# Attention over the keys inside a streaming loop: TensorE sums the weighed values, VectorE normalises the probabilities first and does its pieces of work in another order

## The reference

```python
# B, E, G, P = 64, 16, 5000, 128
W = weight * mask[None, :, :]
h = jnp.einsum('bg,egp->bep', x, W) + bias[None, :, :]
# attention on the normed rows
scores = jnp.einsum('bhqd,bhkd->bhqk', q, k) * scale
scores = jnp.where(mask, scores, jnp.finfo(scores.dtype).min)
attn = jax.nn.softmax(scores, axis=-1)
out = jnp.einsum('bhqk,bhkd->bhqd', attn, v)
h = h + out.transpose(0, 2, 1, 3).reshape(b, s, d) @ W_o.T
# then: top 2 of 64 experts for each row of the normed h, plus two shared experts
```

## Time and profile before

| | |
|---|---|
| median of 3 runs (lowest, highest) | 241.35 us (240.23, 242.11) |
| profiled execution | 241.4 us, span 239.7 us |
| TensorE busy | 184.3 us, 77% |
| VectorE busy | 152.4 us, 64% |
| GpSimd busy | 145.6 us, 61% |
| ScalarE busy | 82.7 us, 35% |
| mean granted TensorE clock | 0.953 of full speed |

### The profile page before, as it was taken

The page is one execution under the profiler, slowest core; times in us unless marked ns, Lnnn a source line. Parts: engine busy times, 40 slices in busy tenths (PEclk is TensorE's granted clock), DMA queues, the critical chain, the costliest instruction groups (busy, mean ns, idle before and its releaser), DMA issues.

```text
span 239.7 us, 6216 instructions
## 1 busy us (share of the span) xinstructions
PE 184.3 (77%) x2549; PEld 154.8 (65%) x2549; DVE 152.4 (64%) x366; ACT 82.7 (35%) x245; POOL 145.6 (61%) x117
## 2 busy tenths in 40 slices
PE   0057969558989969979879789699997989999700
PEld 0056949457878958857758767588776767767400
DVE  0024384686497796897996994978999627410571
ACT  2005200003324324324133124136878744344400
POOL 3326469519998949879969949620161651375360
PEclk9999997977999989999999999999999999999975
DMA  6989999999999999999999999949901329234241
GB/s 220 290 311 417 362 419 384 346 421 415 421 413 417 420 418 420 414 427 418 403 408 228 234 218 191 153 87 303 263 0 44 115 68 296 68 98 121 71 112 35
DMA packets 32982, 65.12 MB, mean 272 GB/s; under 512 B 2874, under 2 KB 25367, under 8 KB 32375
## 3 DMA queue, kind: packets, MB, share of 16 engines
q1 hardware_dynamic: 31416, 59.47, 75.0%
q10 hardware_dynamic: 576, 3.26, 3.4%
q0 software_dynamic: 960, 1.97, 3.1%
HBM read 56.96 MB, written 7.73 MB: 270 GB/s over the span
## 4 chain that ended last, share of the span: by engine, by line
PE 32%; DVE 24%; DMA 18%; SPq 9%; ACT 6%; issue 5%; POOL 3%; POOLq 1%; DVEq 0%; ACTq 0%
DMA ring<-in_L_tok_weight_dram 16%; PE bank L843 10%; DVE ring L1241 5%; SPq L362 4%; DVE bank L1271 4%; PE bank L1045 3%; DVE prod L1262 3%; PE bank L1015 3%; DVE prod L1293 2%; DVE bank L1301 2%; SPq L368 2%; PE bank L993 2%; PE bank L999 2%; PE bank L928 2%; POOL rstd L455 2%
## 5 line engine op out<-in xcount | busy, mean ns | idle before, releaser
L466 POOL TENSOR_TENSOR ring<-ring,mask 128x896 f32<-128x896 f32 (+1 forms) x48 | 91.5, 1935 | 18.7 <-DMA ring<-in_L_tok_weight_dram 18.6
L843 PE MATMUL bank<-ring,xT 128*64 128x128 f32 x1248 | 84.3, 294 | 11.3 <-DVE ring L1241 8.0
L843 PEld LDWEIGHTS bank<-ring,xT 128*64 128x64 f32 x1248 | 76.4, 149 | 16.0 <-DVE ring L1241 12.8
L1241 DVE TENSOR_TENSOR ring<-ring,bank 128x1024 f32<-128x1024 f32 (+1 forms) x45 | 45.8, 1049 | 35.4 <-DMA ring<-in_L_tok_weight_dram 35.4
L455 POOL TENSOR_TENSOR rstd<-mv,half 128x1 f32<-128x1 f32 (+1 forms) x24 | 14.4, 603 | 32.4 <-DVE mv L1249 21.5
L533 POOL DMA_INDIRECT ring<-expert_outputs,slot_index x16 | 16.2, 1010 | 16.6 <-DMA expert_outputs<-ring 12.4
L824 PE MATMUL bank<-cst,w 64*128 64x64 f32 x39 | 5.3, 328 | 15.6 <-DMA w<-in_x_dram 14.8
L486 POOL DMA_INDIRECT expert_inputs<-xf,slot_index x14 | 14.3, 1022 | 4.3 <-issue 3.5
L508 POOL TENSOR_TENSOR mask<-ring,mask 128x256 f32<-128x256 f32 x8 | 7.5, 938 | 14.4 <-ACT ring L705 11.4
L824 PEld LDWEIGHTS bank<-cst,w 64*128 64x128 f32 x39 | 5.0, 219 | 15.7 <-issue 14.8
L579 ACT ACTIVATE offset<-shift,rstd 128x1 f32<-128x1 f32 x16 | 4.7, 292 | 25.1 <-POOL rstd L455 25.1
(11 more groups left out here) (153 smaller groups left out, 297.4 us busy)
## 6 DMA issues: line engine op xcount, KB each, us to landing
ring<-in_L_tok_weight_dram SPq DMA_DIRECT2D x48, 832.0 KB, 13.5
expert_inputs<-w ACTq DMA_DIRECT2D x3, 1024.0 KB, 10.6
ring<-expert_inputs SPq DMA_DIRECT2D x6, 512.0 KB, 5.4
expert_outputs<-ring SPq DMA_DIRECT2D x12, 256.0 KB, 2.7
mask<-in_L_tok_mask_dram SPq DMA_DIRECT2D x3, 832.0 KB, 15.6
w<-in_x_dram SPq DMA_DIRECT2D x1, 1250.0 KB, 13.0
w2p<-in_L_ffn_w_dram SPq DMA_DIRECT2D x1, 1024.0 KB, 19.2
xT<-masks_dram SPq DMA_DIRECT2D x1, 1024.0 KB, 8.1
```

Of the source, the lines that this page charges most:

```text
L466: pool.tensor_tensor(unit(j, q, SPLIT(q // 2), UC), unit(j, q, SPLIT(q // 2), UC), mask[:, (m + SPLIT(q // 2)) * D:(m + UC) * D], ALU.mult ...
L843: last = pe.matmul(bank[0][64 * par:64 * par + 64, 0:D], xT[:, (UC * t + c) * B:(UC * t + c + 1) * B], unit(j, 2 * t + par, c, c + 1), sta ...
L1241: dve.tensor_tensor(both(j, t, a, b), both(j, t, a, b), m.rearrange("p (u f) -> p u f", u=1).to_broadcast([P, 2, (b - a) * D]), ALU.mult). ...
```

## The change

For the chunks 0 to 4 (`IN_LOOP` = 5) VectorE sums the probabilities, takes the reciprocal, multiplies the probabilities by it and then weighs the values; it no longer adds over the positions. TensorE adds: `turn_o` multiplies each of the 2j+2 weighed pieces by the identity, as stationary operand, and sums in PSUM, which gives the transposed heads at once. The keys' multiply of the next chunk waits until that sum is done, because both use `prod`. Chunks 5 to 7 keep the two instructions of `sum_heads`. The values lie as positions x features (`vcat` was features x positions), so that a piece for TensorE is contiguous; ScalarE's copy and both ways of weighing follow that layout, and the sum of chunks 5 to 7 reads with a step of 128 elements.

In a turn VectorE now does three pieces first, then the statistics of chunk a, then the addition for chunk d; one piece each remains in the other places. The spins of turn 6 go and those of turn 7 become four.

```diff
-SPINS = {6: 4, 7: 8}
+SPINS = {7: 4}
+IN_LOOP = NCH - 3
-VECTOR_SHARE = (2, 1, 2, 1)
+VECTOR_SHARE = (3, 1, 1, 1)
...
-        vcat = sb("vcat", [P, D, S])
+        vcat = sb("vcat", [P, S, D])
...
-                act.copy(vcat[:, :, 2 * j:2 * j + 2].rearrange("p f a -> p a f"),
+                act.copy(vcat[:, 2 * j:2 * j + 2, :],
                          bank[3][:, 0:2 * D].rearrange("p (a f) -> p a f", a=2)).then_inc(s_kv, 1)
...
-                pe.transpose(bank[A_BANK(j)][:, 0:P], o[:], ident).then_inc(s_oT, 1)
+                if j >= IN_LOOP:
+                    pe.transpose(bank[A_BANK(j)][:, 0:P], o[:], ident).then_inc(s_oT, 1)
+                    return
+                for s in range(2 * j + 2):
+                    last = pe.matmul(bank[A_BANK(j)][:, 0:P], prod[:, s * D:(s + 1) * D], ident,
+                                     start=s == 0, stop=s == 2 * j + 1)
+                last.then_inc(s_oT, 1)
...
             def multiply_keys(j):
                 n, f = 2 * j + 2, NH * DK
                 dve.wait_ge(s_kv, 2 * j + 2 if j < DIRECT else 2 * j + 1)
+                if 1 <= j <= IN_LOOP:
+                    dve.wait_ge(s_oT, j)
...
-                mark(dve.tensor_reduce(mx[:, 1, :], raw(j).rearrange("p (h s) -> p h s", h=NH), AX.X, ALU.add))
-                then(dve.tensor_tensor(prod[:, 0:n * D].rearrange("p (h d s) -> p h d s", d=DH, s=n),
-                                       vcat[:, :, 0:n].rearrange("p (h d) s -> p h d s", d=DH),
-                                       raw(j).rearrange("p (h a s) -> p h a s", h=NH, a=1).to_broadcast([P, NH, DH, n]),
-                                       ALU.mult))
-                mark(dve.reciprocal(mx[:, 2, :], mx[:, 1, :]))
+                sv = raw(j).rearrange("p (h s) -> p h s", h=NH)
+                weighed = prod[:, 0:n * D].rearrange("p (s h d) -> p s h d", h=NH, d=DH)
+                values = vcat[:, 0:n, :].rearrange("p s (h d) -> p s h d", d=DH)
+                over_values = raw(j).rearrange("p (h s a) -> p s h a", h=NH, a=1).to_broadcast([P, n, NH, DH])
+                if j < IN_LOOP:
+                    then(dve.tensor_reduce(mx[:, 1, :], sv, AX.X, ALU.add))
+                    then(dve.reciprocal(mx[:, 2, :], mx[:, 1, :]))
+                    then(dve.tensor_tensor(sv, sv, mx[:, 2, :].rearrange("p (h a) -> p h a", a=1).to_broadcast([P, NH, n]),
+                                           ALU.mult))
+                    dve.tensor_tensor(weighed, values, over_values, ALU.mult).then_inc(s_o, 1)
+                else:
+                    mark(dve.tensor_reduce(mx[:, 1, :], sv, AX.X, ALU.add))
+                    then(dve.tensor_tensor(weighed, values, over_values, ALU.mult))
+                    mark(dve.reciprocal(mx[:, 2, :], mx[:, 1, :]))
...
-                then(dve.tensor_reduce(o_raw(j), prod[:, 0:n * D].rearrange("p (f s) -> p f s", f=D), AX.X, ALU.add))
+                then(dve.tensor_reduce(o_raw(j), prod[:, 0:n * D].rearrange("p (s f) -> p f s", f=D), AX.X, ALU.add))
...
                 mask_pieces(VECTOR_SHARE[0])
+                if a >= 0:
+                    stats_h(a)
                 if d >= 0:
                     add_attended(d)
...
                 if d >= 0:
                     choose(d)
-                if a >= 0:
-                    stats_h(a)
                 if d >= 0:
                     place(d)
...
                 if b >= 0 and c < NCH - 1:
-                    heads(b)
+                    weigh_values(b)
```

More of the change, by code:

```diff
@@ L1291, in weigh_values @@
                 dve.wait_ge(s_kv, 2 * j + 2)
-                mark(dve.tensor_reduce(mx[:, 1, :], raw(j).rearrange("p (h s) -> p h s", h=NH), AX.X, ALU.add))
-                then(dve.tensor_tensor(prod[:, 0:n * D].rearrange("p (h d s) -> p h d s", d=DH, s=n),
-                                       vcat[:, :, 0:n].rearrange("p (h d) s -> p h d s", d=DH),
-                                       raw(j).rearrange("p (h a s) -> p h a s", h=NH, a=1).to_broadcast([P, NH, DH, n]),
-                                       ALU.mult))
-                mark(dve.reciprocal(mx[:, 2, :], mx[:, 1, :]))
+                sv = raw(j).rearrange("p (h s) -> p h s", h=NH)
[12 more added lines that the diff above has]
+                    mark(dve.reciprocal(mx[:, 2, :], mx[:, 1, :]))
             def sum_heads(j):
                 n = 2 * j + 2
-                then(dve.tensor_reduce(o_raw(j), prod[:, 0:n * D].rearrange("p (f s) -> p f s", f=D), AX.X, ALU.add))
+                then(dve.tensor_reduce(o_raw(j), prod[:, 0:n * D].rearrange("p (s f) -> p f s", f=D), AX.X, ALU.add))
                 dve.tensor_tensor(o[:].rearrange("p (h d) -> p h d", d=DH), o_raw(j).rearrange("p (h d) -> p h d", d=DH),
                                   mx[:, 2, :].rearrange("p (h a) -> p h a", a=1).to_broadcast([P, NH, DH]), ALU.mult).then_inc(s_o, 1)
-            def heads(j):
-                weigh_values(j)
-                sum_heads(j)
             def stats_h(j):
```

## The result

The changed kernel takes 247.8 us (median of 4 runs, 245.35 to 251.02) beside 241.73 (4 runs, 240.23 to 243.15). The ratio is 1.0218, 95% interval 1.011 to 1.033. The profiled execution took 248.04 us around a span of 246.2, against 241.4 around 239.7 before: 6.6 us more. Some executions, here the one of 251.02 us, fell into a slower state with a lower clock; the medians count them and the ratios do not.

What follows compares the result with a forecast made beforehand. The prediction took a dependency circle closing once a turn, not one full engine, to bound the loop, with loads binding up to turn 4. 241.4 + 2.8 (loop) + 2.1 (tail) = 246.3 us, range 242.4 to 248.0.

Steps and rivals of the forecast that it cites:

- The circle: Loop: a dependency chain through VectorE and other engines closes once a turn and binds; addition to next keys' multiply 7.25 us.
- the 1.87 us: VectorE, between heads and addition: one more mask piece (1.12 us) and the statistics (0.75 us) lengthen each turn's chain.
- The rival of VectorE's throughput: Loop: VectorE's total work binds, so savings count in full, 3.9 us; 237.5 us, or 239.6 with slower reads; chance 0.12.
- The turns: Loop, turns 4 to 5, 5 to 6 and 6 to 7: each gets longer, by 0.87, 0.67 and 0.82 us.
- The block: VectorE, turn 5, from the probabilities' sum to the next mask piece: 1.88 us after the change, 2.92 before.
- the 0.45 us of turn 7: TensorE, turn 7: spins and added matmuls outlast VectorE's cover and delay the chain by 0.45 us.
- this way of 3.2 us: TensorE, turn 6, heads to attended rows: 3.2 us with the matmuls, hidden beside 3.6 us of VectorE's pieces and statistics.
- Up to turn 4: Loop until turn 4: later addition costs +0.6 us after 1.3 us free, values' copy gives -0.2, together +0.4 us.
- Earlier turns move under the loads: Turns before turn 4: weight loads bind there, so changes add nothing to the sum.
- the third rival: Loop: the 1.87 us partly hidden, say by faster 52 matmuls in turn 4 or binding loads; 241.5 to 243.2 us; chance 0.12.
- The tail: Behind the loop: VectorE's gapped sums cost +1.5 us for chunk 6, 0.6 for chunk 5, nothing for chunk 7; together +2.1.
- the first rival: Tail: reads with gaps cost VectorE nothing, so 244.2 us; chance 0.25.

Runs made afterwards that it cites:

- run 2: Kernel before with only VectorE's new order, plus 4 to 28 unused identity matmuls on TensorE in turns 3 to 7: 252.06 us; with 2 to 10: 259.58 us.
- run 3: Changed kernel with the old order of VectorE's turn, sums over keys staying on TensorE: 246.0 us, ratio 1.019.
- run 6: Changed kernel with VectorE's old order and the old layout of values and products, so TensorE reads with gaps: 252.64 us, ratio 1.047.
- run b2: Changed kernel with ten unused identity matmuls ahead of the transpose of chunk 6's attended rows, behind the loop: 247.54 us.
- run 5: Changed kernel with the three tail sums reading neighbouring elements (other numbers result): 246.84 us; the same with VectorE's old order: 243.74 us.

## Why the prediction was right, and where its steps were not

The time (247.8 against 246.3) and the sign were right, the time only just: it lies 0.2 us inside the upper end of the range, and the profiled execution, 248.04 us, a little outside. The mechanism of the late turns and of the slower reads is borne out; what happened up to turn 4 and to TensorE in the tail was not in the sum. Point by point:

- **The circle**: right. From the end of the addition to the next keys' multiply it is 134.14 - 127.12 = 7.02 us (7.25 before), and run 2 shows the 1.87 us by themselves, as 1.93, 1.86 and 1.88. The rival of VectorE's throughput is out: VectorE is 4.5 us less busy from 80 to 160 us, and nothing comes of it.
- **The turns**: +0.87, +0.67, +0.82 foreseen, +0.80, +0.54, +0.58 measured. The block (1.88; 1.89), the matmul (0.25; 0.24) and the values' copy (-0.2; -0.23) hold, and the 0.45 us of turn 7 were 0.19. But the sum charges to the order 1.87 us a turn and credits the move with its whole saving. Against before, run 3 has the move at +0.48, +0.08 and +0.57 us, and the order adds +0.32, +0.46 and +0.01: with the old order the addition waits 1.3 to 2.0 us for TensorE. I had set this way of 3.2 us against the cover of the new order alone, and so not seen that it leaves nothing of the saving in any order.
- **Up to turn 4: +0.4**: mis-sized, +1.73 measured. The step that failed is "Earlier turns move under the loads". The moved statistics released GpSimd into the rotation of turn 1, which I had not followed through GpSimd's queue: +2.01 us at turn 2. Turn 3 adds 0.82, which the old order of run 3 doesn't (-0.02): the circle was at work a turn earlier than the sum has it, and from 68 to 110 us VectorE waits for no load any more (0.53, 0.42 and 0.68 us before). 1.10 us came back in turn 4, where the 52 matmuls took 3.06 us and not 4.70, as the third rival had it. That these parts cancel down to 1.73 is luck.
- **The tail: +2.1**: the reduces were 20% cheaper than foreseen (0.67 ns an element against 0.85), 1.20 and not 1.5 us for chunk 6 and 0.56 for 0.6 on chunk 5. Single elements do cost, and the first rival is out. The rule on 16-byte lines in the Trainium skill, SBUF — State Buffer (section Door 1: The DMA port swizzle), agrees with that, and with the weight loads of run 6, which cost nothing more at 8 bytes and all of it from 16 on. What was missing is the wait of 1.46 us that the slower sum opened on TensorE, and a fall of the clock there, 1.1 us by run b2. I had looked for such a fall in turn 7 only. That the wait brings the fall is not shown: run 5 has the fall behind a wait of 0.26 us, in both of its kernels.

By VectorE's last instruction the loop gives +3.65 for 2.8 and the tail +2.5 for 2.1, together 1.3 us short of 6.18.

## What to carry to other kernels

Moving a step to another engine gains only if the way through the new engine is shorter than the step was; compare it from the same start to the same waiting instruction, with the order that would fill the gap kept apart. Of every instruction that moves, follow what it releases: here 0.7 us of statistics released three GpSimd pieces into a row of small VectorE instructions. Look for small VectorE instructions that end with a GpSimd piece in every run of which the time surprises; two runs here lost 5.0 and 2.8 us that way where the slots are given, a place that no expectation had in view. And TensorE's granted clock has a say of its own: it was low behind waits of 2.91, 2.52, 1.46 and 0.74 us, but also behind one of 0.26, and stayed at 1.00 behind one of 0.71. In the tail it costs 1 to 1.5 us in some executions and nothing in others, so a gain of 1 us in one trace has to be read against the spread.

## What was unexpected in the hardware

- VectorE instructions of 0.28 us with two operands in SBUF took 2.04 to 2.17 us beside GpSimd's pieces; its own pieces with one operand in PSUM did not (2.94 us for three, before and after). One of two elements a partition, 0.16 us otherwise, took 6.75 us, through three GpSimd pieces in a row and not one; why is open.
- VectorE pays 0.66 to 0.70 ns for each f32 element read alone 512 bytes apart (1536, 1792 and 2048 elements). TensorE's weight load of 128 such elements takes 192 ns side by side, 194 to 197 at 8 bytes apart, 322 at 40; the whole matmul goes from 0.24 to 0.47 us at 40.
- The same instructions at the same times on TensorE ran at the full clock in one execution and below it in another (1.09 and 1.97 us for 16 matmuls at 175.09 us).
